# Scanning the second half of the context with two matrix products instead of a VectorE scan

## The reference, cut to what matters

```python
# x, ctx: (32, 512, 512); per batch of 512 steps:
r_t = 0.9 * r_(t-1) + ctx_t * ctx_t              # scan over the steps, starts at 0
x = x + layernorm(x) * r
h = layernorm(x) @ W_exp + b_exp                 # 512 -> 2048
h = butterfly(h, up_weights); h = gelu(h + up_bias); h = butterfly(h, down_weights)
x = x + h @ W_con + b_con + down_bias            # 2048 -> 512
```

## Time and profile before

| | |
|---|---|
| median of 3 runs | 2776.57 us (2776.04 to 2776.84) |
| the profiled execution's own time | 2778.74 us |
| its span in the profile | 2776.9 us |
| granted PE clock, mean | 0.994 |
| busy: PE, DVE, ACT, POOL | 99%, 77%, 41%, 15% |
| first `down_a` starts at | 169.03 us |

### The profile page before, as it was taken

The page is one execution under the profiler, slowest core; times in us unless marked ns, Lnnn a source line. Parts: engine busy times, 40 slices in busy tenths (PEclk is TensorE's granted clock), DMA queues, the critical chain, the costliest instruction groups (busy, mean ns, idle before and its releaser), DMA issues.

```text
span 2776.9 us, 34997 instructions
## 1 busy us (share of the span) xinstructions
PE 2735.8 (99%) x12141; PEld 2254.2 (81%) x12141; DVE 2127.3 (77%) x3562; ACT 1140.5 (41%) x1705; POOL 403.8 (15%) x577
## 2 busy tenths in 40 slices
PE   8789999999999999999999999999999999999999
PEld 6668888888888888888888888888888888888887
DVE  8968787787878778787877878777787877778533
ACT  5853434334343433434343343434434343343432
POOL 4721011110101101010110201011020111101000
PEclk8999999999999999999999999999999999999999
DMA  9795665748567575856758585675857657585543
GB/s 266 262 312 163 200 201 174 214 151 254 162 197 204 168 223 155 239 167 194 213 162 231 154 224 183 180 218 160 242 152 221 185 174 224 163 239 153 182 151 99
DMA packets 294837, 542.57 MB, mean 195 GB/s; under 512 B 37430, under 2 KB 101078, under 8 KB 277766
## 3 DMA queue, kind: packets, MB, share of 16 engines
q1 hardware_dynamic: 287760, 536.82, 64.5%
q0 software_dynamic: 1488, 2.27, 0.4%
q10 hardware_dynamic: 5414, 1.25, 0.3%
HBM read 445.83 MB, written 60.82 MB: 182 GB/s over the span
## 4 chain that ended last, share of the span: by engine, by line
PE 94%; DVE 1%; POOL 0%; ACT 0%; issue 0%; DVEq 0%; ACTq 0%; POOLq 0%
PE ps L1715 44%; PE ps L1736 25%; PE ps L1749 25%; PE ps L1610 0%; PE ps L1810 0%; DVE w1r L1171 0%; POOL raw L503 0%; DVE xop L1171 0%; DVE x L1228 0%; ACT xop L897 0%; DVE raw L1225 0%; DVE kvT L1250 0%; DVE kv L1255 0%; DVE st L1231 0%; POOL x L753 0%
## 5 line engine op out<-in xcount | busy, mean ns | idle before, releaser
L1715 PE MATMUL ps<-xop,w1r 128*128 128x512 f32 x5376 | 1363.9, 389 | 5.2 <-ACT st L984 4.4
L1715 PEld LDWEIGHTS ps<-xop,w1r 128*128 128x128 f32 x5376 | 1008.7, 188 | 216.0 <-issue 5.5
L1736 PE MATMUL ps<-w2r,ghi 128*128 128x512 f32 x2048 | 630.5, 389 | 0.0
L1749 PE MATMUL ps<-w2r,ghi 128*128 128x512 f32 x2032 | 625.8, 389 | 0.0
L984 ACT ACTIVATE st<-ps 128x512 f32<-128x512 f32 x384 | 230.0, 599 | 837.2 <-PE ps L1715 837.2
L1365 DVE TENSOR_TENSOR x<-ps,x 128x512 f32<-128x512 f32 x508 | 349.1, 687 | 281.4 <-PE ps L1749 278.9
L1736 PEld LDWEIGHTS ps<-w2r,ghi 128*128 128x128 f32 x2048 | 384.4, 188 | 79.8
L1749 PEld LDWEIGHTS ps<-w2r,ghi 128*128 128x128 f32 x2032 | 381.2, 188 | 79.8 <-DVE glo L1388 0.4
L1383 DVE TENSOR_TENSOR g<-ps,st 128x512 f32<-128x512 f32 x384 | 262.9, 685 | 215.2 <-PE ps L1715 212.0
L988 ACT ACTIVATE g<-g,gelu_bias 128x512 f32<-128x512 f32 x384 | 276.2, 719 | 363.3 <-DVE g L1383 363.3
L1388 DVE TENSOR_TENSOR glo<-g,ghi 128x512 fp32r<-128x512 f32 x510 | 347.9, 703 | 78.8 <-ACT ghi L1002 78.8
(11 more groups left out here) (166 smaller groups left out, 1710.5 us busy)
## 6 DMA issues: line engine op xcount, KB each, us to landing
w1r<-w_products SPq DMA_DIRECT2D x889, 256.0 KB, 3.2
w2r<-w_split SPq DMA_DIRECT2D x126, 1024.0 KB, 4.9
x<-in_x_dram SPq DMA_DIRECT2D x128, 256.0 KB, 7.1
raw<-kv SPq DMA_DIRECT2D x496, 64.0 KB, 2.3
out_dram<-x SPq DMA_DIRECT2D x120, 256.0 KB, 4.1
kv<-in_ctx_dram SPq DMA_DIRECT2D x64, 256.0 KB, 7.4
raw<-in_ctx_dram SPq DMA_DIRECT2D x64, 256.0 KB, 5.3
wexp<-in_L_ffn_W_exp_dram SPq DMA_DIRECT2D x4, 1024.0 KB, 11.1
```

The source lines that it names most:

```text
L1715: last = nc.tensor.matmul(bank[:, :], w1r[:, slot, w, c * P:(c + 1) * P], xop[:, XPOS[m], v, c, :], start=(opens and i == 0), stop=(i == l ...
L1736: last = nc.tensor.matmul(ps_ya[j][:, :], g[:, p % 2, q, j * P:(j + 1) * P], w2r[:, p % 2, kk, w, :], start=(p == 0 and kk == 0 and i == 0 ...
L1749: last = nc.tensor.matmul(ps_yb[:, :], g[:, p % 2, q, j * P:(j + 1) * P], w2r[:, p % 2, kk, w, :], start=(kk == 0 and i == 0), stop=(kk == ...
```

## The change

1. The scan of t = 1 leaves DVE. Two 128x128 matrices are made on DVE (`step_matrices`): one holds the powers of 0.9 within 32 steps, the other carries the last step of the row group before. PE makes each row group j as two plain f32 products of 512 columns into `ps[j]` (`scan_step`). ACT copies the result back for the next group's carry (`keep_step`), and DVE's `gate` reads the scan from PSUM. `scan_step(0)` and `(1)` stand between the last `high_up` steps, `(2)` and `(3)` between and behind the `turn_high` steps.
2. On PE the bias products (`bias_low`, 16 products of one column) come before `turn_high`, not behind it.
3. The `turn_high` evictions and every second `back` eviction go from ACT to DVE.
4. The transfers of h = 0 are all issued by SP, after `scan_step(0)`; POOL's `first_moves(0)` is gone. POOL's `first_moves(1)` goes from behind `weight_sums(6)` to in front of `weight_sums(4)`, and the second bias addition to behind `weight_sums(7)`.
5. SP issues the moves of h = 1 before `store_w1(3)`, not behind `store_w1(5)`. DVE finishes t = 1 before `weights_lo(3)`.
6. Around the first products: `product(0, 0)` goes in front of two `low_dn` steps, `tokens_hi(4)` behind the first copy, and the third copy (`copy(0, 2)`) in front of the first gelu.

```diff
-        FOLD += [("turn_high", q, "act") for q in range(R // 4)]
+        FOLD += [("turn_high", q, "dve") for q in range(R // 4)]
-        FOLD += [("back", k, "act") for k in range(KH)]
+        FOLD += [("back", k, "dve" if k % 2 else "act") for k in range(KH)]
...
             sp.wait_ge(xn_turned, J)
+            sp.wait_ge(step_made, 1)
             move_xT(sp, 0, 0, xT_moved[0])
             move_xT(sp, 0, 1, xT_moved[0])
+            move_xT(sp, 0, 2, first_moved[0])
+            move_xT(sp, 0, 3, first_moved[0])
...
             weight_sums(0)
+            rstd_gated(1, (0, 1))
             weight_sums(1)
-            first_moves(0)
             weight_sums(2)
+            rstd_gated(1, (2, 3))
             weight_sums(3)
-            rstd_gated(1, (0,))
+            first_moves(1)
             weight_sums(4)
-            rstd_gated(1, (1, 2))
             weight_sums(5)
-            rstd_gated(1, (3,))
-            weight_sums(6)
             pool.wait_ge(bias_row_ready, 1)
             add_bias(1, 1, xs[0], (0, 1))
-            first_moves(1)
+            weight_sums(6)
+            weight_sums(7)
             add_bias(1, 1, xs[0], (2, 3))
-            weight_sums(7)
...
+            def keep_step(j):
+                act.wait_ge(step_made, j + 1)
+                act.activation(ctx_rows_of(1)[:, j, :], ps[j][:, :], ACT.Copy).then_inc(step_kept, 1)
...
-            for q in range(R // 4):
-                fold_step("turn_high", q)
-            weights_hi(0)
-            for r in range(3):
-                fold_step("high_dn", r)
+                if r in (R - 3, R - 2):
+                    keep_step(r - R + 3)
+            weights_hi(0, (0, 1))
+            keep_step(2)
+            weights_hi(0, (2,))
             act.activation(yb, ps[4][:, 256:256 + KH], ACT.Copy).then_inc(yb_kept, 1)
+            keep_step(3)
             weights_hi(1)
...
+            def step_matrices():
+                nc.vector.tensor_tensor_scan(out=step_rows[:, :], data0=decay[:, 0:P], data1=ident[:, :], initial=0.0,
+                                             op0=ALU.mult, op1=ALU.add).then_inc(steps_ready, 1)
...
+            step_matrices()
             top_products(1)
-            scan_chunk(1, 1, 0)
-            scan_chunk(1, 1, 1)
-            scan_chunk(1, 1, 2)
-            weights_lo(0)
+            gate(1, 1, xs[0], 0)
+            gate(1, 1, xs[0], 1)
+            for q in range(2):
+                fold_step("turn_high", q)
+            weights_lo(0, (0, 1))
+            gate(1, 1, xs[0], 2)
+            for q in range(2, R // 4):
+                fold_step("turn_high", q)
+            weights_lo(0, (2,))
+            gate(1, 1, xs[0], 3)
+            save_carry(1)
             weights_lo(1)
...
+            def scan_step(j):
+                if j == 0:
+                    pe.wait_ge(low_matrix_ready, 2)
+                    pe.wait_ge(steps_ready, 2)
+                    pe.wait_ge(squared, 2)
+                rows = ctx_rows_of(1)
+                nc.tensor.matmul(ps[j][:, :], step_rows[:, :], rows[:, j, :], start=True, stop=False)
+                pe.wait_ge(step_kept, j + 1)
+                nc.tensor.matmul(ps[j][:, :], carry_rows[:, :], rows[:, j - 1, :] if j else carried_rows,
+                                 start=False, stop=True).then_inc(step_made, 1)
...
+                if r in (R - 3, R - 2):
+                    scan_step(r - R + 3)
...
+            pe.wait_ge(high_matrix_ready, 2)
+            for q in range(2):
+                fold_step("turn_high", q)
+            scan_step(2)
+            for q in range(2, R // 4):
+                fold_step("turn_high", q)
+            scan_step(3)
```

More of the change, by code:

```diff
@@ L257, in xattn_ffn_program @@
         gate_turned = sem("gate_turned")
+        steps_ready = sem("steps_ready")
+        carry_picked = sem("carry_picked")
+        step_made = sem("step_made")
+        step_kept = sem("step_kept")
         stats1_done = sem("stats1_done")
@@ L578, in _ @@
             store_w1(2)
+            sp.wait_ge(xn_turned, 2 * J)
+            move_xT(sp, 1, 0, xT_moved[1])
+            move_xT(sp, 1, 1, xT_moved[1])
             store_w1(3)
@@ L587, in _ @@
             store_w1(6)
-            for i in range(2):
-                store_w2(i)
             store_w1(7)
-            for i in range(2, 5):
+            for i in range(5):
                 store_w2(i)
@@ L919, in _ @@
                     square(0, 0)
+            act.wait_ge(gate_turned, J)
+            act.activation(carried_rows, ctx_rows_of(0)[:, J - 1, :], ACT.Copy).then_inc(step_kept, 1)
             top_hi(1)
@@ L967, in _ @@
             tokens_hi(0, 1, True)
-            for k in range(2, 6):
+            for k in range(2, 4):
+                fold_step("low_dn", k)
+            weights_hi(7)
+            for k in range(4, 6):
                 fold_step("low_dn", k)
@@ L1008, in body @@
                     if first and p == 0:
[L1009 to L1013, removed]
+                        tokens_hi(u, 4, True)
                     if first and p == 2:
@@ L1024, in body @@
                     if first and p == 0:
+                        for k in (W2_BEHIND, W2_BEHIND + 1):
+                            fold_step("low_dn", k)
+                        copy(p, 2, ps_c, 3)
+                        act.wait_ge(w1_stored[0][0], NP // 2 * NX)
+                        act.wait_ge(w1_stored[0][1], NP // 2 * NX)
+                        tokens_hi(u, 6, True)
                         for slot in (W2_APART, 1, 2):
@@ L1040, in body @@
                         tokens_hi(u + 1, 1, False)
-                    copy(p, 2, ps_c, 3)
+                    if not (first and p == 0):
+                        copy(p, 2, ps_c, 3)
                     gelu_summed(p, 1, p + NP)
@@ L1166, in fold_step, with weights_lo @@
                     nc.vector.tensor_copy(*kept(kind, i, bank)).then_inc(fold_kept["dve"], 1)
-            def weights_lo(n):
-                for g, (m0, m1) in enumerate(GROUPS):
+            def weights_lo(n, groups=range(NG)):
+                for g in groups:
                     dve.wait_ge(w1_hi, NG * n + g + 1)
@@ L1222, in gate @@
                     dve.wait_ge(rstd1_ready, t + 1)
-                    dve.wait_ge(gate_turned, t * J + J)
+                    if t != 1:
+                        dve.wait_ge(gate_turned, chunk(t, J))
                     dve.wait_ge(mean1_ready, t * J + J)
-                nc.vector.scalar_tensor_tensor(out=rows, in0=x[:, c, :], scalar=mv1[:, j, 0:1], in1=rows,
+                if t == 0 and j == J - 1:
+                    dve.wait_ge(step_kept, 1)
+                scan = rows
+                if t == 1:
+                    dve.wait_ge(step_kept, j + 2)
+                    dve.wait_ge(xn_turned, J)
+                    wait(dve, x1_ready, n)
+                    scan, rows = ps[j][:, :], kvT[:, :, :].rearrange("p b i -> p (b i)")
+                nc.vector.scalar_tensor_tensor(out=rows, in0=x[:, c, :], scalar=mv1[:, j, 0:1], in1=scan,
                                                op0=ALU.subtract, op1=ALU.mult).then_inc(gated, 1)
@@ L1335, in _ @@
                 fold_step("low_dn", k)
+            weights_lo(7)
             token_sum(0, 0, first=True)
@@ L1766, in body @@
                 if first:
-                    for k in range(W2_BEHIND):
+                    for k in range(W2_BEHIND - 2):
                         fold_step("low_dn", k)
-                    for m in (0, 1, 2, 3):
+                    product(u, 0, 0, first)
+                    for k in (W2_BEHIND - 2, W2_BEHIND - 1):
+                        fold_step("low_dn", k)
+                    for m in (1, 2, 3):
                         product(u, 0, m, first)
```

67 lines of the change are left out of this document (44 added, 23 removed).

## The result

The changed kernel takes 2790.22 us (median, 2789.32 to 2791.11); the kernel before took 2776.31 us on the same chip. The ratio is 1.0047, with a 95% interval of 1.0035 to 1.0059. So the change makes the kernel slower, by 13.9 us between the medians. The predicted 2778 and its range up to 2784 were both too low.

The account below looks back on a forecast made before the run. ACT, then DVE and POOL, bound the stretch before the first `down_a` (S). First `tokens_hi` (T0) at 135.4 plus 35.1 put S at 170.5 us, 1.5 later; with 2.2 us off for the profiled execution, 2778 us, range 2770 to 2784.

Parts of the forecast that it names:

- the shared `back` evictions: Before the first `tokens_hi`: moving half of the 16 `back` evictions to DVE takes 3.8 us from ACT, partly given back.
- The added work until `high_dn`: On PE, scan steps, bias products and `turn_high` delay the start of `high_dn` by 9.7 us, called the cost of the change.
- 1.1 us, as a quarter of a 1.23 us scan each: On DVE before `top_products(1)`: `step_matrices`, two scans over 128 columns and two small instructions, plus gaps, priced at 1.1 us.
- POOL's moved transfers in front of `weight_sums(4)`: POOL waits for tokens until 111 us, ends `weight_sums(4)` at 119.1; ACT's `weights_hi(4)` ends 5.7 us late; case's chance 0.5.
- POOL isn't late: Rival: `weights_hi(4)` ends at 114.5 us, the first `down_a` starts at 164.9, time 2772.5 us; chance 0.25.
- From `weights_hi(4)` to T0: From the end of `weights_hi(4)` at 120.2 us to the first `tokens_hi`, forecast at 135.4 us, 9.3 later than before.
- followed bank by bank this gives back 1.3 us twice: Around `weights_lo(5)` and `(6)`: DVE's late copies and PE's three-bank limit return 1.3 us twice of ACT's 3.8 us saving.
- From T0 to S: From the first `tokens_hi` to the first `down_a`: 35.1 us against 43.0, with POOL's late `weights_hi(7)` wait gone.
- the way to the first product: From the first `tokens_hi` to `product(0, 0)`: forecast at 14 us.
- the low clock covers the scan steps: Rival: 16 scan instructions on PE take 0.44 us more each; first `down_a` at 176.2, time 2783.8 us; chance 0.12.
- Transfers set S: Rival: stores of `w_split` and loads of `w1r` hold the first `down_a` at 169, time 2776.6 us; chance 0.13.
- the expected gain: On DVE: tokens of t = 1 are turned at 111 us instead of 127.6, 16.6 us earlier, with SP's and POOL's moves.

Follow-up runs that it names:

- e5: The changed kernel with `step_matrices` ahead of the first scan of t = 0; ratio 1.0026 to the kernel before.
- e7: The changed kernel with POOL's transfers behind `weight_sums(6)`, bias additions last, SP's h = 1 moves behind `store_w1(4)`, all `back` evictions on ACT, `step_matrices` early; ratio 0.9989.
- e9: e7's kernel with the odd `back` evictions on DVE again; ratio 0.9997 to the kernel before.
- e12: e7's kernel with SP's order of the change, h = 1 moves ahead of `store_w1(3)` and `store_w1(4)`; median 2780.80 us, ratio 1.0009 to the kernel before.
- e1: The changed kernel with POOL's eight h = 1 transfers behind `weight_sums(5)` instead of in front of `weight_sums(4)`; ratio 1.0044 to the kernel before.
- e2: e1's kernel with all sixteen `back` evictions on ACT again; ratio 1.0038 to the kernel before.
- e11: e7's kernel with `step_matrices` back where the change has it, beside POOL's addition; median 2782.05 us, ratio 1.0014 to the kernel before.
- e3: The kernel before with part 6 of the change alone, the reordering around the first products; ratio 0.9995 to the kernel before.
- e4: The changed kernel with the bias products behind `scan_step(3)`, `keep_step(2)` and `(3)` before `weights_hi(0)`, `weights_lo(0)` behind the last gate; ratio 1.0051 to the kernel before.
- e6: The changed kernel with each scan product cut to 16 of its 512 columns; ratio 1.0041 to the kernel before.
- e10: e7's kernel with the 32 one-column bias products behind the last scan step; median 2773.36 us, ratio 0.9988 to the kernel before.
- e8: e3's kernel with `weight_sums(7)` ahead of the second pair of bias additions; median 2774.54 us, ratio 0.9993 to the kernel before.

## Why the prediction was wrong

The chain that was forecast is the one in the profile: ACT late behind POOL's moved transfers, and everything behind ACT late with it. Three terms of its sum were wrong, all in one direction, and one of them, the shared `back` evictions, had the wrong sign.

- *The added work until `high_dn`.* From step 0 to `high_dn` 17.3 us were forecast and 17.4 measured, with the low clock in the bias products (4.74 us, forecast 4.8). That part was exact, but partly by luck, since it hangs on when the clock falls: the same work took 15.7 us in e5, e7 and e9 and 14.0 in e12.
- *`step_matrices`, "1.1 us, as a quarter of a 1.23 us scan each": wrong, it held DVE for 4.3 us* (73.25 to 77.56). The failed step is the small instruction in it: 3.37 us beside POOL's 3.75 us instruction, 0.17 us alone at 33.37 in e5. It began 0.4 us after POOL's and both ended within 0.03 us of each other. The forecast looked at the size of the instruction and not at what ran beside it on POOL. With it, top to step was 3.3 us longer than forecast, and moving it in e5 took 5.7 us off S, 3.8 of it up to step 0. The Trainium skill (SBUF — State Buffer, Who interferes with whom) says that a `tensor_scalar` can enter a two-port mode if its operands meet some conditions, that VectorE and GpSimd share one pair of ports, and that whoever issues first holds it for its whole instruction. The trace agrees in 3.37 against 0.17 us; the rule should have been in the sum. That it was POOL and not the place in DVE's queue was not tried by itself.
- *POOL's moved transfers in front of `weight_sums(4)`.* Counted from dn, `weight_sums(4)` ends after 24.9 us (forecast 24.5), and ACT's wait was 6.5 us (forecast 5.7). The rival "POOL isn't late" is excluded.
- *From `weights_hi(4)` to T0: 15.2 us forecast, 19.5 measured* (123.3 to 142.8). The failed step is the term for the halved `back` evictions: 3.8 us taken from ACT, and "followed bank by bank this gives back 1.3 us twice". With all sixteen on ACT the durations of the sum give 15.9 us, and 15.8 were measured in e7; shared, it took 19.7 in e9 and 19.5 here. So the sharing, forecast to shorten this stretch by 0.7 us (the difference of 15.9 and 15.2; its stated terms, 3.8 less 2.6, would make it 1.2), goes with 3.9 us more, of which 2.9 lie behind `weights_hi(5)`, where PE waits for DVE's copies. DVE's copies stand behind `weights_lo(5)` and `(6)`; these follow ACT and are slow beside POOL's bias additions (2.58 and 2.28 us where the same shapes took 1.02 and 1.22 at 116 and 115 us), and PE then stands before a full bank. The low clock behind PE's pause is a smaller share: `turn_low` took 3.5 us to the start of `back`, in e1 without that pause 2.7. The Trainium skill (TensorE: Matmul & The Clock Gate, Part 1) says that the lower rate is the default and that PE's activity releases it; the trace agrees here, at 0.8 us, and the forecast had weighed this rule and left it out.
- *From T0 to S: 35.1 forecast, 37.4 measured.* The step that failed is the way to the first product: 14 us forecast, 16.0 measured, while the rest was 21.1 and 21.4. Behind the pause of 3.02 us at 141.57 the clock was low again (0.57 from 142 to 146 us), and the first four `low_dn` instructions took 3.38 us. In e2, e11 and e12, where the first four took 1.95 to 2.00 us, the same way took 14.3 to 14.5 (15.3 in e7, where ACT waited 1.55 us for a token sum on it). Part 6 is worth 3.1 of the 5.6 us gained here (e3); no pause of 3.85 us is left, as forecast.

The errors add up: 3.3 + 4.3 + 2.3 = 9.9 us, 0.3 at POOL and 0.1 up to `high_dn`, less 0.55 because the head of this execution was earlier: about 9.6, which is S = 180.1 against 170.5. The other 2.6 us to the median come mostly from taking 2.2 off for the profiled execution before. The changed kernel's own one (2789.6) lay only 0.6 below its median.

Of the rivals, "the low clock covers the scan steps" named the right side and half the size (2783.8), but not the cause: steps 0 and 1 ran at 0.86 to 0.97 us a product, start to start, with the granted clock at 1.00, and only step 2 ran at the low one. "Transfers set S" is excluded as stated: S was to be held at 169, and it came at 165.0 in e7. A transfer does matter in e1, e2 and e12, as a store of a staging slot for which ACT waits. Such a wait stood in the kernel before too, within the stretch of which the prediction says that ACT has hardly a pause:

```profile
117.19 1.06 ACT L882 ACTIVATE w1r<-stmp 128x1024 fp32r<-128x1024 f32 x1 [2.19 <-DMA w_products<-w1r]
```

Where did the expected gain go? The last transposition of the tokens of t = 1 began 13 us earlier (113.8 against 126.9 us). But they bound the end only in the kernel before. The path had moved to ACT, which began 12.6 us later, and what it and PE wanted stood in three queues behind work that waited: POOL's sums and SP's stores behind the wait for the tokens, DVE's copies behind `weights_lo`, which waits for ACT itself. In e7 the same scan on TensorE, with these three orders undone and the matrices early, costs nothing: top to S is 95.5 us, 15.7 under the changed kernel and as short as e3's 95.7 without it. (The 99.6 of the kernel before holds 1.3 us of low clock that e3 didn't have.) So the scan on TensorE has not been shown to gain anything over part 6 alone; what it does not do is cost, once the orders fit.

## What to carry to other kernels

When a change makes one engine's result earlier, moving its consumers forward in the queues is only safe if nothing behind them in the same queue is wanted by another engine at that time; check each of POOL, SP and DVE for what stands behind the new wait. Work that depends on constants alone belongs where its engine is otherwise alone, however small it is: price a small instruction by what runs beside it. Compare executions from a landmark that the change doesn't touch, since here the head alone moved by up to 6 us.

## What the runs showed of the hardware

- A 128x4 `TENSOR_SCALAR` on DVE took 3.37 us in the changed kernel and 0.17 us elsewhere, and ended with POOL's 128x2048 addition. The value was 3.37 or 3.38 us in each of the six profiles in which both were together (changed, e1, e2, e4, e6, e11), and 0.17 in the five with early matrices (e5, e7, e9, e10, e12). In all six it began 0.4 us behind POOL's, so no other overlap was seen.
- The first product of step 0 took 1.12 or 1.13 us behind pauses of PE of up to 2.2 us (changed, e1, e5, e7, e9, e10, e12), 1.33 behind 4.42 us (e4), and 2.07 behind 5.02 and 5.61 us (e2, e11), with the granted clock at its lower level, 1.2 GHz. In the changed kernel and e1 the clock had been low before, at 74 to 77 us behind a pause of 2.15 and 2.02 us, where PE had to wait for DVE anyway. From top to `high_dn` they took 28.5 and 28.6 us, e2 and e11, with the one long pause, 29.4 and 29.2.
- The 32 one-column bias products took 3.63 to 3.81 us in nine profiles and 4.25 to 4.92 in five (before, changed, e1, e8, e10). In e12 the granted clock stayed at 1.00 from 80 to 100 us, in the changed kernel it was 0.50 from 88 to 94.
